# Four passes over gathered rows: every tile gathered by GpSimd, none by SyncE's one-row transfers

## The chip, the cores and the metric

The kernel runs on one core of one Trainium2 chip. The metric is the device time of one execution in microseconds (us); the profile is a separate execution, taken by the hardware profiler. Engines are named as in the profile: PE (TensorE matmul), PEld (its weight load), DVE (VectorE), ACT (ScalarE), POOL (GpSimd) and SP (SyncE). SP computes nothing: it issues transfers and passes semaphores on.

## The reference

Four graph layers work one after the other on 12500 nodes of 128 features, with the same 200000 edges, which are sorted by their destination `dst`:

```
h = relu(layernorm(x)); x = x + GCN(h)          # two convolutions: 128 -> 256 -> 128
h = relu(layernorm(x)); x = x + L1(h)           # total - segment_sum(h[src], dst), normalised, linear
h = relu(layernorm(x)); x = x + weightedGCN(h)  # edge weights in the messages and in the degrees
h = relu(layernorm(x)); x = x + GAT(h)          # projections of both ends, batch norm, silu, edge softmax
```

What costs time is in each layer `segment_sum(rows[src], dst)`: for each edge a row of a table in HBM, by a random number `src`, is fetched, and rows with one destination are added up.

## The kernel before

The edges are cut into 1563 tiles of 128 edges (`NT`). A gather fetches one tile: an indirect DMA, issued by POOL, whose 128 partitions each receive the row that one number of `idx_tab` names. The kernel has five passes over all tiles (numbers 0 to 4), each in a block of its own, with a barrier of all engines between blocks:

- passes 0, 1 and 2 (`pass_in_parts`) fetch from `table16`, whose rows of 384 bf16 numbers (768 bytes) hold each value in three parts. ACT builds one-hot matrices, PE multiplies them with the rows into PSUM windows of 128 nodes, DVE evicts windows;
- pass 3 (`pass_with_weights`) fetches 512-byte rows of `table`; DVE builds the weighted one-hot matrices, ACT evicts;
- pass 4 fetches 520-byte rows of `ptable` and sends its sums to HBM; a last block multiplies them out, then come the final norm and the output.

Between the passes stand short blocks with the layers' linear algebra and norms, which store the next table.

In a pass tiles go in groups of eight (`GT`), 196 groups (`TGROUPS`), through a ring in SBUF of eight groups (`RGROUPS`; four in pass 4). Three engines keep the ring going:

- POOL (`gather_tiles`) issues a group's gathers one by one; from group 8 on it first waits until `s_free` says that the slots are empty;
- SP (`relay_rows`) waits until a group has landed and counts it up in `s_landed`, two groups (`LEAD`) ahead, for PE; then it waits until PE's products of the oldest group are done and counts `s_free` up, for POOL;
- PE waits for `s_landed` every eight products.

In passes 0 to 3 POOL doesn't fetch all tiles. Of each sixth group from the eighth on (`SIDE`: 31 groups, 8 to 188) it leaves out the last tile. SP fetches that tile's 128 rows by 128 transfers of one row each (`side_rows`), cut into six portions of some 21 rows, one after each `s_free` that it gives: it loads 32 row numbers at once into registers (line 502, four loads for a tile), and each transfer (line 506) takes its address from one of them. The numbers come from two small tables in SBUF (`side_of`), which the first block loads and multiplies by the row's size (lines 835, 973 and 975). SP waits for the tile by a semaphore of its own (`s_side`, line 470), clears it (line 471) and only then hands the group over (line 472).

Of the kernel before, what the change touches and what calls it, by code (L numbers as in the profile page):

```python
# [5 lines left out]
P = 128  # L6
F = 128
GT = 8
SLOTS = 4 * GT
READY_STEP = 4  # L10
RGROUPS = 8
LEAD = 2
SIDE_FIRST, SIDE_EVERY = 8, 6
SIDE_LOAD = 32
Z_RGROUPS = 4
# [3 lines left out]
NPARTS = 3  # L19
# [37 lines left out]
def gnn_kernel(nc, x, src, dst, edge_weight, node_vec1, L0_W1, L0_b1, L0_W2, L0_b2, L1_W, L1_b, L2_W, L2_b,  # L57
# [21 lines left out]
    NTAB = NI + BODY  # L79
    SIDE = list(range(SIDE_FIRST, TGROUPS - RGROUPS + LEAD + 1, SIDE_EVERY))  # L80
    SIDE_SPAN = SIDE_EVERY * GT * P
    SIDE_BASE = (SIDE_FIRST + 1) * GT * P - SIDE_SPAN
    assert SIDE_FIRST == RGROUPS and RGROUPS - SIDE_EVERY == LEAD and SIDE_BASE + len(SIDE) * SIDE_SPAN <= E
    CHUNKS = NW // CW
# [24 lines left out]
    with ctx:  # L109
# [76 lines left out]
        score_tab = ew_tab[:, 0:NI]  # L186
        side_tab = sb("side_numbers", [64 + len(SIDE), P], i32)
        side_of = [side_tab[64 * k:64 * k + len(SIDE), :] for k in range(2)]
        rows_all = sb("rows", [13, max(7 * SCW, NI // 2, PLAN_HALVES * PLAN_WORDS)])
# [247 lines left out]
        s_free = sem("rows_free")  # L437
        s_side = sem("side_rows")

        def tiles_of(g):  # L440
            return min(GT, NT - g * GT)

        def has_side(no, g):

            return no < PASSES - 1 and g in SIDE

        def landed_count(no, g):

            return 16 * sum(tiles_of(k) - has_side(n, k) for n in range(no + 1)
                            for k in range(g % RGROUPS, g + 1 if n == no else TGROUPS, RGROUPS))  # L450

        def gather_tiles(pool, no, tab, slots, groups, width):

            freed = no * (TGROUPS - RGROUPS)
            for g in range(TGROUPS):
                if g >= groups:
                    pool.wait_ge(s_free, freed + g - groups + 1)
                for k in range(tiles_of(g) - has_side(no, g)):
                    t = g * GT + k
                    pool.indirect_dma_start(  # L460
                        out=slots[:, t % (groups * GT), 0:width], out_offset=None, in_=tab,
                        in_offset=bass.IndirectOffsetOnAxis(ap=idx_tab[:, t // P, t % P:t % P + 1], axis=0),
                    ).then_inc(gathered[g % RGROUPS], 16)

        def relay_rows(sp, no, groups, lead, s_done, done0, fetch_side=None):

            def landed(g):
                sp.wait_ge(gathered[g % RGROUPS], landed_count(no, g))
                if has_side(no, g):
                    sp.wait_ge(s_side, 16 * P)  # L470
                    sp.sem_clear(s_side)
                sp.sem_inc(s_landed[no], 1)  # L472

            for g in range(lead):
                landed(g)
            for g in range(TGROUPS):
                if g + lead < TGROUPS:
                    landed(g + lead)
                if g + groups < TGROUPS:
                    if g % 4 == 0:  # L480
                        releases = table_values(sp, RELEASE, g, 4, NI)
                    sp.wait_ge(s_done, releases[g % 4] + done0)
                    sp.sem_inc(s_free, 1)
                    if fetch_side:
                        fetch_side(sp, g)

        def side_rows(no, tab, slots, width, kind, row_bytes):

            flat, size = tab.rearrange("n f -> (n f)").unsqueeze(0), row_bytes // width

            numbers = []

            def fetch(sp, g):
                k, j = g // SIDE_EVERY, g % SIDE_EVERY
                if k >= len(SIDE):
                    return
                t = SIDE[k] * GT + GT - 1
                for e in range(j * P // SIDE_EVERY, (j + 1) * P // SIDE_EVERY):
                    if e % SIDE_LOAD == 0:
                        numbers.clear()  # L500
                        words = [nc.alloc_registers(f"side{no}_{k}_{e + i}", engines=[SP]) for i in range(SIDE_LOAD)]
                        nc.regs_load(words, side_of[kind][k:k + 1, e:e + SIDE_LOAD])
                        numbers.extend(nc.snap(word, engines=[SP], donate=True, min_val=0, max_val=(N - 1) * row_bytes,
                                               guaranteed_mod_val=0, out_of_modulus=row_bytes) for word in words)
                    at = numbers[e % SIDE_LOAD] // size
                    sp.dma_start(slots[e:e + 1, t % RSLOTS, 0:width], flat[:, bass.ds(at, width)]).then_inc(s_side, 16)

            return fetch

# [61 lines left out]
        def pass_in_parts(no, from_acc, sums_of, finish, count_weights=False):  # L571
# [3 lines left out]
            with nc.Block() as block:  # L575
# [4 lines left out]
                @block.sync  # L580
                def _(sp):
                    relay_rows(sp, no, RGROUPS, LEAD, s_prod, items0, side_rows(no, table16, ring16, NPARTS * F, 0, 2 * NPARTS * F))

# [72 lines left out]
        def pass_with_weights(no):  # L656
# [3 lines left out]
            with nc.Block() as block:  # L660
# [4 lines left out]
                @block.sync  # L665
                def _(sp):
                    relay_rows(sp, no, RGROUPS, LEAD, s_prod, items0, side_rows(no, table, ring32, F, 1, 4 * F))

# [96 lines left out]
        with nc.Block() as block:  # L765
# [58 lines left out]
            def _(sp):  # L824
# [6 lines left out]
                else:  # L831
                    sp.sem_inc(s_last, 16)
                side_src = src[SIDE_BASE:SIDE_BASE + len(SIDE) * SIDE_SPAN].rearrange("(k s) -> k s", s=SIDE_SPAN)[:, SIDE_SPAN - P:]
# [52 lines left out]
            def _(act):  # L886
# [65 lines left out]

                act.wait_ge(s_dve, 16)
                nc.scalar.activation(deg_r, deg, ACT.Sqrt).then_inc(s_cnt, 1)
# [9 lines left out]
            def _(dve):  # L964
# [25 lines left out]
                dve.wait_ge(s_starts, 1)  # L990
                step = Steps(dve, s_dve, 4, 10)
                step(nc.vector.tensor_tensor(bound[:, 0:NW], bank[5][:, 0:NW], wplus1[:, 0:NW], ALU.add))
# [82 lines left out]

                step = Steps(dve, s_dve, 4 + 10, 3)
                dve.wait_ge(s_degrees, 1)
# [18 lines left out]
            def _(pe):  # L1096
# [5 lines left out]
                last.then_inc(s_counted, 1)  # L1102
                pe.wait_ge(s_dve, 4)
                nc.tensor.matmul(bank[5][:, 0:NW], first, tile_cnt[:, 1:NW + 1], start=True, stop=True).then_inc(s_starts, 1)
# [886 lines left out]
```

## Time and profile before

| | |
|---|---|
| time of an execution, median of 3 | 14196.16 us (14169.2 to 14197.04) |
| profiled execution, first to last instruction | 11157.3 us |
| POOL busy | 8098.3 us, 73% of the span |
| PE, PEld busy | 4270.1 us (38%), 2948.2 us (26%) |
| DVE, ACT busy | 3430.3 us (31%), 3212.6 us (29%) |
| gathers (DMA_INDIRECT, line 460) | 4596 + 1532 + 1563 |
| one-row transfers (line 506) | 11904 + 3968 |

The profiled execution's own time is known as its span alone; what lies around it isn't in the profile. The median of the three timed executions is 3038.9 us above the span. The busy shares are means over passes and the blocks between them, so a bound has to be read stage by stage. What SP issues isn't counted as busy, nor is POOL's sequencer between two gathers.

### The profile page before, as it was taken

How to read it: one execution, taken by the hardware profiler on the slowest of the kernel's cores; microseconds unless marked ns; L12 is line 12 of the kernel's file. 1: busy time of each engine (PE TensorE's matmuls, PEld its weight loads, DVE VectorE, ACT ScalarE, POOL GpSimd, SP SyncE). 2: the span in 40 equal slices, each digit the busy share in tenths (PEclk: the TensorE clock that was granted, in tenths of full speed). 3: DMA queues.
4: the chain of work that ended last, by engine and by line, in shares of the span. 5: the costliest groups of instructions: out<-in, count | busy, mean ns of one | idle time of the engine just before them, and what ended most of it. 6: DMA issues, size and time to landing. Idle time of an engine off the chain costs nothing. (4 is left out here: it accounts for less than half of the span.)

```text
span 11157.3 us, 112702 instructions
## 1 busy us (share of the span) xinstructions
PE 4270.1 (38%) x19462; PEld 2948.2 (26%) x19462; DVE 3430.3 (31%) x7386; ACT 3212.6 (29%) x7261; POOL 8098.3 (73%) x8241
## 2 busy tenths in 40 slices
PE   1222222342222233333333433343464333443687
PEld 0111111121111112111111333333353333333576
DVE  4000001110001112000001422222245677777898
ACT  3333333343333334333333300000031111111465
POOL 4777777657777775777777677777766777777676
PEclk5555555665555555555555555556675555555899
DMA  4333333233333333333333222222214555555444
GB/s 105 81 81 81 81 81 81 76 88 81 81 81 81 81 81 102 81 81 81 81 81 81 59 54 54 54 54 54 54 48 148 159 162 163 166 166 170 149 167 134
DMA packets 702798, 1071.72 MB, mean 96 GB/s; under 512 B 164740, under 2 KB 547065, under 8 KB 675209
## 3 DMA queue, kind: packets, MB, share of 16 engines
q0 software_dynamic: 323616, 664.87, 23.0%
q10 hardware_dynamic: 247712, 225.10, 6.1%
q1 hardware_dynamic: 130793, 174.77, 4.9%
q14 instruction: 501, 4.10, 0.1%
q8 instruction: 176, 2.88, 0.1%
HBM read 904.67 MB, written 161.05 MB: 96 GB/s over the span
## 5 line engine op out<-in xcount | busy, mean ns | idle before, releaser
L460 POOL DMA_INDIRECT big<-table_parts,tile_cols x4596 | 4348.0, 946 | 1563.2 <-issue 1400.2
L641 PE MATMUL psum<-big 128*128 x4992 | 1722.0, 505 | 3998.4 <-SPq L472 3044.2
L641 PEld LDWEIGHTS psum<-big 128*128 128x128 bf16 x4992 | 670.0, 141 | 4980.6 <-issue 2814.6
L460 POOL DMA_INDIRECT big<-ptable,tile_cols x1563 | 1496.6, 957 | 498.4 <-issue 476.0
L460 POOL DMA_INDIRECT big<-table,tile_cols x1532 | 1454.6, 949 | 469.5 <-issue 467.0
L596 ACT ACTIVATE big<-big,ones 128x2048 bf16<-128x2048 bf16 x312 | 624.4, 2001 | 3573.5 <-PE psum L641 2381.1
L589 ACT ACTIVATE big<-iota_col,dl_tab 128x128 bf16<-128x128 f32 x4992 | 1490.7, 387 | 32.9 <-PEq L765 12.5
L1656 PE MATMUL psum<-acc,big 128*128 x3328 | 785.0, 419 | 1205.5 <-DVE big L1632 1193.4
L618 DVE TENSOR_REDUCE acc<-psum 128x128 f32<-128x384 f32 (+1 forms) x196 | 109.7, 560 | 3558.1 <-PE psum L644 1783.4
L713 PE MATMUL psum<-big 128*128 x3328 | 754.6, 419 | 1158.3 <-SPq L472 619.7
L1656 PEld LDWEIGHTS psum<-acc,big 128*128 128x128 f32 x3328 | 701.8, 315 | 1288.5 <-issue 1288.2
L713 PEld LDWEIGHTS psum<-big 128*128 128x128 f32 x3328 | 704.8, 323 | 1209.5 <-SPq L472 534.3
L676 DVE TENSOR_SCALAR big<-iota_col,dl_tab,ew_tab 128x128 f32<-128x128 f32 x1664 | 438.8, 365 | 1476.1 <-PE psum L713 1469.4
L1609 DVE TENSOR_REDUCE wide<-big 128x128 f32<-128x2048 f32 x208 | 766.1, 3683 | 3.2 <-ACT big L1683 3.2
L1632 DVE SCALAR_TENSOR_TENSOR big<-big,sc,psum 128x130 f32<-128x130 f32 x1664 | 515.9, 343 | 552.9 <-SPq L472 294.7
L618 DVE TENSOR_REDUCE big<-psum 128x128 f32<-128x384 f32 x98 | 54.7, 558 | 1722.2 <-PE psum L641 1722.1
L692 ACT COPY acc<-psum 128x128 f32<-128x128 f32 x98 | 26.0, 266 | 1858.4 <-PE psum L713 1849.0
L1868 PE MATMUL psum<-big 128*128 128x129 f32 x3328 | 543.4, 297 | 38.5 <-POOL big L1789 36.5
L1788 POOL TENSOR_TENSOR big<-big,tile_cols 128x2048 f32<-128x2048 f32 x104 | 376.0, 3615 | 119.4 <-ACT big L1829 119.2
L1868 PEld LDWEIGHTS psum<-big 128*128 128x128 f32 x3328 | 425.1, 193 | 68.2 <-issue 52.7
L1683 ACT ACTIVATE big<-big 128x2048 f32<-128x2048 f32 x104 | 199.6, 1920 | 712.1 <-DVE wide L1613 707.6
L644 PE MATMUL psum<-big 128*128 128x3 bf16 x1664 | 352.5, 212 | 0.0
(301 smaller groups left out, 4278.8 us busy)
## 6 DMA issues: line engine op xcount, KB each, us to landing
big<-table_parts SPq DMA_DIRECT2D x11904, 0.8 KB
big<-dl_rows ACTq DMA_DIRECT2D x104, 1024.0 KB
zrows<-big ACTq DMA_DIRECT2D x104, 1024.0 KB, 5.5
big<-zrows SPq DMA_DIRECT2D x104, 1024.0 KB, 4.9
big<-table_parts,tile_cols POOLq DMA_INDIRECT x4596
big<-table SPq DMA_DIRECT2D x3968, 0.5 KB
table_parts<-big SPq DMA_DIRECT2D x42, 672.0 KB, 3.5
big<-ptable,tile_cols POOLq DMA_INDIRECT x1563
```

The lines of the kernel that those rows point to most:

```text
L460: pool.indirect_dma_start(out=slots[:, t % (groups * GT), 0:width], out_offset=None, in_=tab, in_offset=bass.IndirectOffsetOnAxis(ap=idx_t ...
L589: last = nc.scalar.activation(apart_flat[:, u * P:(u + 1) * P], iota_col[:], ACT.Abs, bias=dl_tab[:, col:col + 1], scale=-1.0)
L596: nc.scalar.activation(half, apart_flat, ACT.Relu, bias=ones[:, 0:1], scale=-1.0).then_inc(s_onehot, 1)
L641: last = nc.tensor.matmul(held, m, rows_t, start=False, stop=False, skip_group_check=True)
L644: last = nc.tensor.matmul(held, m, ew_parts[:, q * HALF + u, :], start=False, stop=False, skip_group_check=True)
L676: last = nc.vector.tensor_scalar(wide_onehot[:, q % 2 * HALF + u, :], iota_col[:], dl_tab[:, col:col + 1], ew_tab[:, col:col + 1], ALU.is_ ...
L713: last = nc.tensor.matmul(held, wide_onehot[:, q % 2 * HALF + u, :], rows_t, start=False, stop=False, skip_group_check=True)
L1609: nc.vector.tensor_reduce(part[:, k, :], rows_of, AX.X, ALU.add).then_inc(s_part, 1)
L1632: last = nc.vector.scalar_tensor_tensor(zbuf[:, h, u, 0:ACW], dyn(ring_flat, slots[u], ACW), in_win[:, h, u:u + 1], bank[n % Z_BANKS][:, 0 ...
L1656: last = nc.tensor.matmul(bank[n % Z_BANKS][:, 0:ACW], onehot_t[:, q % 2, u * P:(u + 1) * P], dyn(acc_flat, at[u], ACW), start=True, stop= ...
L1788: nc.gpsimd.tensor_tensor(m[:, :, 0:F], m[:, :, 0:F], over_f(weights_of(q), HALF), ALU.mult)
L1868: nc.tensor.matmul(dyn(sums_at, at[u], SCW), onehot[:, q % 2 * HALF + u, :], msg[q % MSGS][:, u, 0:SCW], start=False, stop=False, skip_gro ...
```

## The change

POOL gathers all tiles of all groups in all passes. `relay_rows` only hands groups over and slots back. `side_rows`, its registers, semaphore and two number tables go, and with them their two loads and two multiplications in the first block. Counts of semaphores that those steps had raised are lowered to match. Nothing of what PE, ACT or DVE compute in the passes changes.

```diff
 def landed_count(no, g):
-    return 16 * sum(tiles_of(k) - has_side(n, k) for n in range(no + 1)
+    return 16 * sum(tiles_of(k) for n in range(no + 1)
                     for k in range(g % RGROUPS, g + 1 if n == no else TGROUPS, RGROUPS))
 ...
     for g in range(TGROUPS):
         if g >= groups:
             pool.wait_ge(s_free, freed + g - groups + 1)
-        for k in range(tiles_of(g) - has_side(no, g)):
+        for k in range(tiles_of(g)):
 ...
-def relay_rows(sp, no, groups, lead, s_done, done0, fetch_side=None):
+def relay_rows(sp, no, groups, lead, s_done, done0):
     def landed(g):
         sp.wait_ge(gathered[g % RGROUPS], landed_count(no, g))
-        if has_side(no, g):
-            sp.wait_ge(s_side, 16 * P)
-            sp.sem_clear(s_side)
         sp.sem_inc(s_landed[no], 1)
 ...
             sp.wait_ge(s_done, releases[g % 4] + done0)
             sp.sem_inc(s_free, 1)
-            if fetch_side:
-                fetch_side(sp, g)
-
-def side_rows(no, tab, slots, width, kind, row_bytes):
-    ...
-                nc.regs_load(words, side_of[kind][k:k + 1, e:e + SIDE_LOAD])
-    ...
-            sp.dma_start(slots[e:e + 1, t % RSLOTS, 0:width], flat[:, bass.ds(at, width)]).then_inc(s_side, 16)
 ...
-                for to in side_of:
-                    sp.dma_start(to, side_src).then_inc(s_last, 16)
 ...
-                dve.wait_ge(s_last, 64)
-                nc.vector.tensor_scalar(side_of[0], side_of[0], 2 * NPARTS * F, None, ALU.mult)
-                step = Steps(dve, s_dve, 0, 4)
-                step(nc.vector.tensor_scalar(side_of[1], side_of[1], 4 * F, None, ALU.mult))
+                dve.wait_ge(s_last, 32)
+                step = Steps(dve, s_dve, 0, 3)
```

On POOL, in the middle of pass 0, this stands before: gathers of 128 rows of 384 numbers, the first of each group behind its wait for `s_free` (rows_free).

```order
L460 DMA big<-table_parts,tile_cols 128x384 x7
L460 DMA big<-table_parts,tile_cols 128x384 [waits rows_free]
L460 DMA big<-table_parts,tile_cols 128x384 x6
L460 DMA big<-table_parts,tile_cols 128x384 [waits rows_free]
L460 DMA big<-table_parts,tile_cols 128x384 x7
```

And now, at the same place (line 447 of the changed kernel is the same gather):

```order
L447 DMA big<-table_parts,tile_cols 128x384 x7
L447 DMA big<-table_parts,tile_cols 128x384 [waits rows_free]
L447 DMA big<-table_parts,tile_cols 128x384 x7
L447 DMA big<-table_parts,tile_cols 128x384 [waits rows_free]
L447 DMA big<-table_parts,tile_cols 128x384 x7
```

The group that had seven gathers has eight; this comes 31 times in a pass.

On SP, also in pass 0, this stands before: 64 transfers of one row, number loads, the hand-over waits (`gathered0` to `gathered7` are the semaphores of the gathers' groups, `product_done` that of PE).

```order
L512 TENSOR_LOAD rows [waits gathered6]
L506 DMA big<-table_parts 1x384 [waits product_done]
L506 DMA big<-table_parts 1x384 x10
L502 TENSOR_LOAD side_numbers
L506 DMA big<-table_parts 1x384 x10
L506 DMA big<-table_parts 1x384 [waits gathered7,product_done]
L506 DMA big<-table_parts 1x384 x21
L471 ISA [waits side_rows,gathered0]
L502 TENSOR_LOAD side_numbers [waits product_done]
L506 DMA big<-table_parts 1x384 x21
```

And now, where line 471 of the changed kernel is what was line 512:

```order
L471 TENSOR_LOAD rows [waits product_done,gathered7,gathered0,gathered1,gathered2]
L471 TENSOR_LOAD rows [waits product_done,gathered3,gathered4,gathered5,gathered6]
L471 TENSOR_LOAD rows [waits product_done,gathered7,gathered0,gathered1,gathered2]
L471 TENSOR_LOAD rows [waits product_done,gathered3,gathered4,gathered5,gathered6]
L471 TENSOR_LOAD rows [waits product_done,gathered7,gathered0,gathered1,gathered2]
```

Between two loads of four release numbers nothing is left on SP but the waits and counts.

## Rows read from the trace of the kernel before

**Rows 1.** The stages: us of the window, busy time (x instructions), PEclk, DMA share, GB/s.

```profile
267.00:2183.00 1916.00, 570.42 (x1671) 218.59 (x1670) 126.78 (x388) 704.37 (x1767) 1449.22 (x1532) 0.55 0.30 81
2307.00:4222.00 1915.00, 571.92 (x1671) 218.98 (x1670) 172.82 (x580) 703.96 (x1765) 1448.11 (x1532) 0.55 0.30 81
4284.00:6202.00 1918.00, 611.90 (x3327) 303.83 (x3328) 109.83 (x290) 704.84 (x1768) 1450.29 (x1532) 0.54 0.30 81
6324.00:8247.00 1923.00, 764.93 (x3326) 706.70 (x3327) 438.58 (x1664) 51.38 (x194) 1454.61 (x1532) 0.59 0.21 54
8394.00:10368.00 1974.00, 779.57 (x3306) 696.93 (x3307) 1419.95 (x2681) 230.43 (x308) 1496.57 (x1563) 0.57 0.56 163
```

**Rows 2.** Line 460, the gathers of each pass: min/median/max ns, first and last start.

```profile
L460 POOL DMA_INDIRECT big<-table_parts,tile_cols x1532: 942/946/1317, 267.0 to 2182.0; - x192
L460 POOL DMA_INDIRECT big<-table_parts,tile_cols x1532: 942/946/1045, 2306.6 to 4220.9; - x192
L460 POOL DMA_INDIRECT big<-table_parts,tile_cols x1532: 942/946/1445, 4284.5 to 6200.5; - x192
L460 POOL DMA_INDIRECT big<-table,tile_cols x1532: 940/944/1089, 6324.4 to 8245.1; - x192
L460 POOL DMA_INDIRECT big<-ptable,tile_cols x1563: 940/944/1213, 8394.5 to 10366.1; - x196
```

**Rows 3.** What POOL waited for: us in total, times, longest.

```profile
POOL big L460 <- issue: 2343.2, 7686, 0.3
POOL big L460 <- POOLq L765: 63.0, 1, 63.0
```

**Rows 4.** POOL in order of time, in pass 0 and at its end.

```profile
999.61 0.95 POOL L460 DMA_INDIRECT big<-table_parts,tile_cols  x1 [0.30 <-issue]
1000.86 0.95 POOL L460 DMA_INDIRECT big<-table_parts,tile_cols  x1 [0.30 <-issue]
...
2181.95 0.95 POOL L460 DMA_INDIRECT big<-table_parts,tile_cols  x1 [0.30 <-issue]
2190.67 6.84 POOL L1159 TENSOR_TENSOR big<-acc,dinv 128x896 f32<-128x896 f32 x3 [7.77 <-POOLq L575]
```

**Rows 5.** SP's one-row transfers and number loads, whole trace.

```profile
L506 SPq DMA_DIRECT2D big<-table_parts x11904: 219/225/342, 301.7 to 6138.5; - x199
L506 SPq DMA_DIRECT2D big<-table x3968: 224/225/338, 6359.4 to 8182.7; - x199
L502 SPq TENSOR_LOAD <-side_numbers x496: 1865/2124/2383, 299.6 to 8169.7; - x166
```

**Rows 6.** SP in order of time in pass 0: a run without a load, and a long stretch.

```profile
999.86 1.81 SPq L506 DMA_DIRECT2D big<-table_parts  x6
939.78 126.35 SPq L506 DMA_DIRECT2D big<-table_parts  x272
```

**Rows 7.** What SP waited for between 900 and 2100 us.

```profile
SPq L472 <- DMA big<-table_parts,tile_cols: 92.7, 83, 2.9
SPq L470 <- DMA big<-table_parts: 27.3, 20, 1.7
```

**Rows 8.** What PE waited for in pass 0.

```profile
PE psum L641 <- SPq L472: 993.7, 140, 8.0
PE psum L641 <- issue: 219.8, 34, 7.7
PE psum L641 <- SPq L471: 131.4, 22, 6.3
```

**Rows 9.** DVE at the start of the first block, in order of time.

```profile
4.71 0.59 DVE L971 TENSOR_SCALAR is_node<-node_id 128x98 f32<-128x98 f32 x1 [3.62 <-POOL big L789]
6.47 0.21 DVE L973 TENSOR_SCALAR side_numbers<-side_numbers 31x128 int32<-31x128 int32 x1 [1.17 <-DMA side_numbers<-in_src]
6.95 0.17 DVE L976 TENSOR_SCALAR big<-big 128x13 int32<-128x13 int32 x1
```

More of the change, by code:

```diff
@@ L12 @@
 LEAD = 2
-SIDE_FIRST, SIDE_EVERY = 8, 6
-SIDE_LOAD = 32
 Z_RGROUPS = 4
@@ L79, in gnn_kernel @@
     NTAB = NI + BODY
[L80 to L83, printed above, removed]
     CHUNKS = NW // CW
@@ L186, in gnn_kernel @@
         score_tab = ew_tab[:, 0:NI]
-        side_tab = sb("side_numbers", [64 + len(SIDE), P], i32)
-        side_of = [side_tab[64 * k:64 * k + len(SIDE), :] for k in range(2)]
         rows_all = sb("rows", [13, max(7 * SCW, NI // 2, PLAN_HALVES * PLAN_WORDS)])
@@ L437, in gnn_kernel @@
         s_free = sem("rows_free")
-        s_side = sem("side_rows")
         def tiles_of(g):
             return min(GT, NT - g * GT)
-        def has_side(no, g):
-            return no < PASSES - 1 and g in SIDE
         def landed_count(no, g):
-            return 16 * sum(tiles_of(k) - has_side(n, k) for n in range(no + 1)
+            return 16 * sum(tiles_of(k) for n in range(no + 1)
                             for k in range(g % RGROUPS, g + 1 if n == no else TGROUPS, RGROUPS))
@@ L483, in relay_rows @@
                     sp.sem_inc(s_free, 1)
-                    if fetch_side:
-                        fetch_side(sp, g)
-        def side_rows(no, tab, slots, width, kind, row_bytes):
[L489 to L501, printed above, removed]
-                        nc.regs_load(words, side_of[kind][k:k + 1, e:e + SIDE_LOAD])
-                        numbers.extend(nc.snap(word, engines=[SP], donate=True, min_val=0, max_val=(N - 1) * row_bytes,
-                                               guaranteed_mod_val=0, out_of_modulus=row_bytes) for word in words)
-                    at = numbers[e % SIDE_LOAD] // size
-                    sp.dma_start(slots[e:e + 1, t % RSLOTS, 0:width], flat[:, bass.ds(at, width)]).then_inc(s_side, 16)
-            return fetch
         def table_values(eng, tab, start, n, largest):
@@ L581, in _ @@
                 def _(sp):
-                    relay_rows(sp, no, RGROUPS, LEAD, s_prod, items0, side_rows(no, table16, ring16, NPARTS * F, 0, 2 * NPARTS * F))
+                    relay_rows(sp, no, RGROUPS, LEAD, s_prod, items0)
                 @block.scalar
@@ L666, in _ @@
                 def _(sp):
-                    relay_rows(sp, no, RGROUPS, LEAD, s_prod, items0, side_rows(no, table, ring32, F, 1, 4 * F))
+                    relay_rows(sp, no, RGROUPS, LEAD, s_prod, items0)
                 @block.vector
@@ L832, in _ @@
                     sp.sem_inc(s_last, 16)
-                side_src = src[SIDE_BASE:SIDE_BASE + len(SIDE) * SIDE_SPAN].rearrange("(k s) -> k s", s=SIDE_SPAN)[:, SIDE_SPAN - P:]
-                for to in side_of:
-                    sp.dma_start(to, side_src).then_inc(s_last, 16)
                 sp.wait_ge(s_pad, 4)
@@ L951, in _ @@
                         ln.relu(act, t - 1, (t - 1) % 2)
-                act.wait_ge(s_dve, 16)
+                act.wait_ge(s_dve, 15)
                 nc.scalar.activation(deg_r, deg, ACT.Sqrt).then_inc(s_cnt, 1)
@@ L990, in _ @@
                 dve.wait_ge(s_starts, 1)
-                step = Steps(dve, s_dve, 4, 10)
+                step = Steps(dve, s_dve, 3, 10)
                 step(nc.vector.tensor_tensor(bound[:, 0:NW], bank[5][:, 0:NW], wplus1[:, 0:NW], ALU.add))
@@ L1074, in _ @@
                         keep_dl(t - 2)
-                step = Steps(dve, s_dve, 4 + 10, 3)
+                step = Steps(dve, s_dve, 3 + 10, 3)
                 dve.wait_ge(s_degrees, 1)
@@ L1102, in _ @@
                 last.then_inc(s_counted, 1)
-                pe.wait_ge(s_dve, 4)
+                pe.wait_ge(s_dve, 3)
                 nc.tensor.matmul(bank[5][:, 0:NW], first, tile_cnt[:, 1:NW + 1], start=True, stop=True).then_inc(s_starts, 1)
```

## The prediction

> **What bounds the kernel now.** I read the stages first, then what ends the waits of each engine in them; the chain of waits on the page covers only the last block and says nothing of the passes. The reader is to see in the stages [rows 1] that four windows of 1915 to 1923 us have the same number of gathers, 1532, and very different work on the other engines: PE goes from 570 to 765 us, ACT from 704 down to 51, DVE from 110 up to 439. Their lengths don't follow any of it. They follow POOL: 1448 to 1455 us busy in all four. The DMA engines have a share of 0.21 to 0.30 there, and of 0.56 in pass 4, so they aren't the bound.
>
> The gathers themselves [rows 2] give the pitch from one to the next: (2182.0 - 267.0) / 1531 = 1.2508 us in pass 0, 1914.3 / 1531 = 1.2504 in pass 1, 1916.0 / 1531 = 1.2515 in pass 2, 1920.7 / 1531 = 1.2545 in pass 3 and 1971.6 / 1562 = 1.2622 in pass 4, which has no one-row transfers beside it. A pitch is 0.95 us of gather and 0.30 us of its own sequencer [rows 4]. What POOL waited for [rows 3] has 7686 such gaps of at most 0.3 us put down to issue, one wait at the barrier before pass 0, and no wait for `s_free`: the ring of eight groups never runs full. And the pass ends right behind POOL: its next instruction in the next block starts 7.8 us after its last gather [rows 4]. So in passes 0 to 3 the path is POOL's chain of gathers, and one gather more is one pitch more.
>
> SP is the second in line. A one-row transfer takes 0.225 us [rows 5], but six take 1.81 us, so the pitch between them is (1.81 - 0.225) / 5 = 0.317 us [rows 6]. A tile costs SP 128 x 0.317 + 4 x 2.124 us of number loads [rows 5] = 49.1 us. POOL gives it 47 gathers for that (six groups of eight less one): 47 x 1.251 = 58.8 us. SP is used to 84% by this alone; over a long stretch it issues 272 rows in 126.35 us, 59.5 us for 128 [rows 6], POOL's own pace, and it waits 120 of 1200 us, nearly all of it for landings [rows 7]. It keeps up. PE's waits that end with SP's lines 472 and 471 [rows 8] are only the hand-over of rows that PE has long been free for.
>
> **The change part by part.**
>
> Added: 31 gathers in each of four passes. In passes 0 to 2, 3 x 31 x 1.251 = 116.3 us; in pass 3, 31 x 1.2545 = 38.9 us. Together 155.2 us. The lower bound for a pitch is a gather alone, 0.94 us [rows 2], should the sequencer's gap hide (124 x 0.94 = 117 us), the upper the pitch of pass 4 (124 x 1.2622 = 156.5 us). I take 155, since every gather in those passes has its gap. Nothing hides it: POOL has no wait to give up.
>
> Removed on SP: 15872 one-row transfers, 496 number loads and 124 clears. They lie beside POOL's chain and are worth 0 there. Could their going make POOL's pitch shorter? The nearest rows say no: the median gather is 946 ns in passes 0 to 2, 944 in pass 3 and 944 in pass 4 without them. At the most 2 ns x 4596 = 9 us come back; I take 0, because pass 3 has them too and shows 944.
>
> What is late next: SP hands over a group as soon as its last gather has landed, where it might first have had up to 21 rows to issue. PE gets rows a little sooner, and still waits for POOL: it is busy 570 to 765 us of some 1920 [rows 1]. Slots are given back sooner; POOL doesn't wait for them. The last side group is the 188th, so the end of a pass is as before.
>
> In the first block two loads and two multiplications go. DVE waits 1.17 us for the side numbers, and from the end of line 971 (5.30) to line 976 (6.95) 1.65 us could go, if the last numbers of `dst` have landed by then [rows 9]; between 0 and -1.65 us I take -1.
>
> The sum is +154 us: the profiled execution would go from 11157.3 to about 11311 us. That span is 3038.9 us below the median of the timed executions, and the trace doesn't tell where those lie. I take them as unchanged: 14196 + 154 = 14350 us. If instead all of them lay in the gathers' pitch, it would be 1.251 + 3038.9 / 7691 = 1.646 us in the timed executions, and the 124 gathers 204 us: 14400 us. That is the other end for the same mechanism.
>
> On this the Trainium skill's page "Runtime: NRT & Kernel Launch" (The ~15µs preamble/postamble breakdown) has about 9 to 15 us around a kernel. The 3038.9 us here are two hundred times that; by that rule most of them lie inside the execution, which speaks for the higher end and also for the first rival below.
>
> **The rivals.**
>
> B, faster: SP, not POOL, sets the pace in the timed executions. The place is the portion of 21 rows before each hand-over. SP decides as soon as a tile costs it more than 58.8 us, that is from (58.8 - 8.5) / 128 = 0.393 us a row, 24% above the 0.317 us of the trace. Were all the 3038.9 us due to it, a tile would cost 58.8 + 3038.9 / 124 = 83.3 us, 0.584 us a row, and with the transfers gone the time would fall to 11157.3 + 154, about 11310 us; at half of it, 12830 us. For it speaks that SP has only 16% in reserve and that 3 ms have no place yet. Against it: in the trace SP waits 10% of the time and POOL never waits for slots [rows 3, 7], the 15872 transfers vary only from 219 to 342 ns [rows 5], and nothing shown makes an execution without the profiler slower in SP alone.
>
> The Trainium skill's page "DMA: Bandwidth & Descriptors" gives 512 sequencer cycles for such a transfer on this generation (section "Why a DMA increments its semaphore by 16 and not by 1", its table's column on previous generations), which at the 1.2 GHz of the Trainium skill's page "Trainium Kernel Development and Optimization" (NeuronCore Architecture) is an estimate of 0.427 us, beyond the 0.393 of the rival; the trace has 0.225 us, and here the measurement decides.
>
> C, no change: the gathers' issue isn't what binds, or less of it. To leave the time alone POOL's pitch would have to fall to 1.251 x 1532 / 1563 = 1.226 us once SP's rows are off the DMA queues, and the time would be 14195 us. For it: the one-row transfers share the DMA engines with the gathers. Against it: that share is 0.30, and pass 4 has the same gather of 944 ns at a share of 0.56 and no row transfers [rows 1, 2].
>
> The Trainium skill's page "DMA: Bandwidth & Descriptors" also says (Issuing engines are not separate DMA queues) that issuing from several engines at once only saves the sequencer's issue time, usually small beside the transfer. By that rule the side rows were worth little and C would hold; in the trace issue is the larger part, 1.25 us of every gather at a DMA share of 0.30.
>
> That the change doesn't do what it says is excluded by the order: eight gathers stand where seven stood.
>
> **How the numbers follow.** The forecast, slower by 154 to 204 us, gets 0.80; B 0.11; C 0.09. The predicted time is 14350 us. A measurement of this kernel can't tell less than about 0.2% (28 us) from no change. The forecast's own range is 14310 to 14430 us: 154 less the 38 us of the hidden gaps and a little for the median, up to 204 and the same. That holds about 0.76; to leave out no more than 2 in 10 I reach down over C, to 14180. The range is 14180 to 14430 us; B lies outside. Faster by over 0.2%: B's 0.11 and 0.02 of C, 0.13. Within 0.2%: the rest of C, 0.07. Slower: 0.80.
>
> **What the profile of the changed kernel would show.** Right: 1563 gathers in each of the first four passes, at a pitch of 1.25 us, windows of about 1954 to 1962 us instead of 1915 to 1923, POOL's idle time still put down to issue, pass 4 as before, no line 502 or 506, and the first gather at about 266 us. SP would wait for landings nearly all the time. Wrong: a pitch of 1.23 us or less (C); waits of POOL for slots, which would mean that PE or SP had become the bound; or a span of about 11311 us with a timed median that falls towards it, which would show that the missing 3 ms were SP's (B). A span of about 11311 us and a timed median some 200 us higher would put them into the gathers.

## The result and the profile after

The changed kernel took 12869.92 us (median of 4 runs, 12863.67 to 12872.75) beside 14186.72 us for the kernel before (4 runs, 14169.2 to 14197.04). The ratio is 0.9069, 95% interval [0.9052, 0.9086]: faster by 9.3%, where 1.1% slower was forecast, and far below the range.

One thing has to be known to read any number below. The same kernel before takes 11156 to 11189 us in some jobs on the chips and 14187 to 14201 us in others (medians), and all its runs of one job lie within about 0.5%. A job is one session on one chip, in which several kernels are timed beside one another. I call these the 11.2 jobs and the 14.2 jobs. The timed runs of the forecast come from a 14.2 job, the profile of before from an 11.2 job. A ratio is always to runs of before in the same job, and where times of different jobs are compared, the jobs are of one kind.

The windows of the five passes of the changed kernel in its 14.2 job, with the columns of [rows 1]:

```profile
279.00:2479.00 2200.00, 493.77 (x1664) 206.48 (x1662) 122.69 (x380) 707.59 (x1764) 1480.34 (x1563) 0.56 0.26 70
2606.00:4808.00 2202.00, 495.83 (x1664) 207.67 (x1664) 166.36 (x564) 707.55 (x1767) 1480.37 (x1563) 0.56 0.26 70
4875.00:7100.00 2225.00, 545.20 (x3248) 281.02 (x3248) 104.61 (x281) 693.01 (x1740) 1484.46 (x1563) 0.57 0.26 69
7232.00:9450.00 2218.00, 639.41 (x3269) 585.75 (x3270) 426.54 (x1632) 49.78 (x189) 1481.31 (x1563) 0.60 0.18 47
9609.00:12064.00 2455.00, 786.14 (x3280) 701.31 (x3280) 1407.14 (x2662) 228.28 (x305) 1490.60 (x1563) 0.55 0.45 131
```

The number of gathers rose from 1532 to 1563 as forecast, but a pass takes 2200 to 2225 us, not 1954 to 1962. The gathers themselves are what they were in [rows 2]:

```profile
L447 POOL DMA_INDIRECT big<-table_parts,tile_cols x4689: 940/946/1440, 278.9 to 7099.2; - x196
L447 POOL DMA_INDIRECT big<-table,tile_cols x1563: 938/944/1094, 7233.0 to 9449.4; - x196
L447 POOL DMA_INDIRECT big<-ptable,tile_cols x1563: 938/944/1221, 9609.8 to 12063.1; - x196
```

What is new is a wait that [rows 3] does not have, first on POOL, then on SP, with total, times and longest ("remote": the trace doesn't show which engine's instruction ended the wait):

```profile
POOL big L447 <- issue: 2319.3, 7512, 2.5
POOL big L447 <- SPq L467: 1560.5, 298, 17.5
```

```profile
SPq L467 <- remote: 6835.6, 407, 48.9
SPq L467 <- DVE big L1586: 1462.9, 145, 25.6
```

POOL waits 1560.5 us for slots that SP gives back at line 467, and SP waits at its wait for PE's count, where in [rows 7] it waited for landings. The prediction named this as the mark of "wrong".

The same two views of the kernel before in a 14.2 job (run e15, 14201.13 us) were the missing piece, since the profile that the forecast was read from is of the other kind of job:

```profile
279.00:2854.00 2575.00, 561.81 (x1648) 215.16 (x1648) 123.02 (x379) 696.72 (x1751) 1456.85 (x1532) 0.54 0.23 60
2983.00:5532.00 2549.00, 560.34 (x1648) 214.80 (x1648) 165.80 (x560) 695.93 (x1750) 1455.53 (x1532) 0.54 0.23 61
5604.00:8153.00 2549.00, 601.03 (x3248) 297.30 (x3246) 105.27 (x280) 692.57 (x1739) 1457.19 (x1532) 0.53 0.23 61
8287.00:10800.00 2513.00, 754.20 (x3262) 696.06 (x3262) 428.80 (x1632) 50.13 (x189) 1453.62 (x1532) 0.56 0.16 41
10954.00:13400.00 2446.00, 786.43 (x3281) 701.83 (x3282) 1411.75 (x2665) 228.46 (x306) 1499.29 (x1563) 0.55 0.45 131
```

```profile
POOL big L460 <- SPq L483: 3004.2, 591, 17.4
POOL big L460 <- issue: 2207.7, 7026, 2.0
```

So the 3038.9 us lay inside the passes. Against [rows 1], passes 0 to 3 take 659, 634, 631 and 590 us more, pass 4 takes 472 more, all the rest 56: 3042 us. POOL is as busy as in [rows 1] (1457 for 1449 us in pass 0) and waits 3004.2 us for slots, which is nearly the whole difference. The change then takes 375, 347, 324 and 295 us off passes 0 to 3, 1341 us, and nothing off pass 4 (2455 for 2446) or outside the windows (1566.9 for 1567.4). So the spans differ by 1332.5 us, and the medians at the top by 1317.

SP's rows in the 14.2 job, first between 900 and 2100 us and then over the whole trace (min/median/max ns):

```profile
L506 SPq MOVE big<-table_parts x1932: 1/29/1409, 900.0 to 2099.9; - x194
L506 SPq DMA_DIRECT2D big<-table_parts x1932: 1/228/1421, 900.1 to 2099.9; - x194
```

```profile
L506 SPq DMA_DIRECT2D big<-table_parts x11904: 1/228/1421, 317.2 to 8135.7; - x199
```

and in an 11.2 job, between the same times:

```profile
L506 SPq MOVE big<-table_parts x2610: 29/29/38, 902.3 to 2099.8; - x187
L506 SPq DMA_DIRECT2D big<-table_parts x2610: 224/225/318, 902.4 to 2099.8; - x187
```

The reader is to see that the medians hardly differ (228 for 225 ns) and the number of rows does: 1932 against 2610 in the same 1200 us, 0.621 us a row with all that SP does beside it. The longest of a transfer is 1421 ns where it was 342 [rows 5]. SP is not slower all the time: from one transfer to the next it takes 322 ns in the median, where it was 318, but it halts again and again. Of its 4060 steps from one instruction to the next in this stretch, those behind a load left out, 411 take 0.6 to 0.8 us and 148 take 1.3 to 1.5 us, against 15 and 17 in the profile of before (counted from the traces' records). SP has 12.2 us of waits in that stretch, where it had 120 [rows 7]:

```profile
SPq L470 <- DMA big<-table_parts: 12.2, 11, 1.4
```

SP is full, and a tile costs it 128 x 0.621 = 79.5 us, number loads and halts included, while POOL would need 58.8 us for the six groups.

### The profile page after: what moved, and what is told of

The parts are those of the page before. It is cut to its first block and busy times, and to the rows that moved or that the text cites. A ratio compares the mean times of both kernels' runs of the same rounds, so it can differ in the third digit from the quotient of the medians.

```text
span 12866.9 us, 80456 instructions
## 1 busy us (share of the span) xinstructions
PE 3963.6 (31%) x19462; PEld 2811.3 (22%) x19462; DVE 3421.9 (27%) x7384; ACT 3223.1 (25%) x7261; POOL 8214.4 (64%) x8365
## 5 line engine op out<-in xcount | busy, mean ns | idle before, releaser
L447 POOL DMA_INDIRECT big<-table_parts,tile_cols x4689 | 4445.7, 948 | 2348.6 <-issue 1398.7
L600 PE MATMUL psum<-big 128*128 x4992 | 1507.0, 459 | 5013.4 <-issue 2719.2
L447 POOL DMA_INDIRECT big<-table,tile_cols x1563 | 1481.7, 948 | 738.2 <-issue 468.6
L600 PEld LDWEIGHTS psum<-big 128*128 128x128 bf16 x4992 | 628.2, 131 | 5806.9 <-issue 4232.7
L672 PE MATMUL psum<-big 128*128 x3328 | 638.9, 365 | 1583.0 <-issue 876.4
L672 PEld LDWEIGHTS psum<-big 128*128 128x128 f32 x3328 | 592.8, 273 | 1630.5 <-issue 1271.9
L1822 PEld LDWEIGHTS psum<-big 128*128 128x128 f32 x3328 | 427.6, 194 | 66.5 <-issue 51.3
```

Source lines behind the costliest of these rows:

```text
L447: pool.indirect_dma_start(out=slots[:, t % (groups * GT), 0:width], out_offset=None, in_=tab, in_offset=bass.IndirectOffsetOnAxis(ap=idx_t ...
L600: last = nc.tensor.matmul(held, m, rows_t, start=False, stop=False, skip_group_check=True)
L672: last = nc.tensor.matmul(held, wide_onehot[:, q % 2 * HALF + u, :], rows_t, start=False, stop=False, skip_group_check=True)
L1822: nc.tensor.matmul(dyn(sums_at, at[u], SCW), onehot[:, q % 2 * HALF + u, :], msg[q % MSGS][:, u, 0:SCW], start=False, stop=False, skip_gro ...
```

## Experiments

**Are the time and the sum reproducible: the kernel before, unchanged (e1, e13, e15), and the changed kernel again (e5).** No edit.

> The kernel before, unchanged. Question: where do the 3039 us stand by which its timed executions exceed its profiled span? Theory H (hand-over): in the timed executions the counts of PE's finished products reach SP late, POOL waits for slots, and SP's portions of 21 row transfers lengthen each turn; then the span here is near 14190 us, gathers keep their median of 0.95 us, and POOL waits some 3000 us for SP's line 472 in the passes. Rival O (outside): the span is again about 11160 us and the rest lies around it. Rival P (pitch): the span is near 14190 and the gathers' own pitch is 1.6 us.

> The kernel before. Where it takes 14187 us, theory R (instructions and counts of all engines drain at a limited rate there) expects SP's own instructions stretched to some 0.7 us in bursts, as the half-reduced version showed, about 2500 us a pass, POOL with some 3000 us of waits for slots, and few of the counts' records; the gathers still at 0.95 us. Where it takes 11187, as e1.

> As e13. Where it takes 14187 us: POOL waits some 3000 us for slots, SP's instructions are stretched to some 0.7 us in bursts, a pass takes about 2500 us.

> The changed kernel, unchanged, beside the kernel before. In the last call the kernel before took 11187 us, its profiled span, where it had taken 14187 us beside the changed kernel; so the time of one and the same kernel differs by 27% between jobs. Theory S (a state of the chip or of the job in which semaphore counts come late, not a property of the kernels): if the kernel before is near 11187 us here, the changed one is 155 us above it, near 11342 us, as the version with LEAD = 6 was, and POOL has no waits for slots; if the kernel before is near 14187, the changed one is near 12870 again. Rival K (the changed kernel itself makes the counts late, since SP waits instead of issuing): 12870 us whatever the kernel before takes.

Before took 11186.67 us (ratio to the runs of before beside it 1.0 [0.999, 1.0009]), 11155.69 (0.9998) and 14201.13 (1.0001 [0.9986, 1.0016]). So both kinds of jobs are stable, and the kernel is the same in them. The profiled execution of e15 took 14201.16 us, no longer than its other seven. e1 expected a 14.2 job and its marks; they came with e15: 3004 us of waits, gathers at 949 ns (median) and not at a pitch of 1.6 us. The changed kernel in an 11.2 job: 11348.87 us beside 11187.68, ratio 1.0143 [1.0126, 1.016], 161 us more where the sum said 154. (Between the two profiled executions it is 188.6 us, 178 of them in passes 0 to 3 and 11 in pass 4.) Its passes 0 and 4 and POOL's gaps before its gathers:

```profile
267.00:2231.00 1964.00, 568.81 (x1671) 217.58 (x1672) 126.78 (x388) 704.81 (x1768) 1487.23 (x1563) 0.55 0.29 78
8570.00:10555.00 1985.00, 781.59 (x3304) 698.84 (x3304) 1419.54 (x2679) 230.24 (x306) 1508.19 (x1563) 0.57 0.56 162
```

```profile
POOL big L447 <- issue: 2381.4, 7810, 0.3
```

The change has the opposite sign in the two kinds of jobs. There is no wait for slots here, as the prediction's own marks of "right" had it.

**Gathers and transfers both (e3, e10, e14, e16).** The kernel before, but POOL gathers every tile, and SP still issues all 15872 one-row transfers, 320 bytes each, into memory that nobody reads:

```diff
+        side_dump = sb("side_dump", [P, 160], bf16)
 ...
-            return 16 * sum(tiles_of(k) - has_side(n, k) for n in range(no + 1)
+            return 16 * sum(tiles_of(k) for n in range(no + 1)
 ...
-                for k in range(tiles_of(g) - has_side(no, g)):
+                for k in range(tiles_of(g)):
 ...
-                    sp.dma_start(slots[e:e + 1, t % RSLOTS, 0:width], flat[:, bass.ds(at, width)]).then_inc(s_side, 16)
+                    sp.dma_start((side_dump[e:e + 1, :] if width > F else side_dump[e:e + 1, :].bitcast(f32)), flat[:, bass.ds(at, 160 if width > F else 80)]).then_inc(s_side, 16)
```

> POOL gathers every tile, as in the changed kernel, and SP issues its 15872 row transfers as before, at the same places and with the same number loads and waits, but into a scratch tile and of 320 bytes each; nobody uses them. Theory H: the row transfers cost their time on SP, so this is as slow as before plus at most the 155 us of the 31 gathers a pass: 14200 to 14400 us. Rival: what the change gains comes from somewhere else than SP's transfers (the tile's landing, say, that PE no longer waits for): near 12900.

> POOL gathers every tile and SP issues the 15872 row transfers into a scratch tile. 11344 us where the kernel before takes 11187, as much as the changed kernel without them. Where it takes 14187: theories R and T1 both say that the transfers cost what they cost before, plus the 124 gathers: 14340 us; if the late landing of a tile that PE waits for was the cost, 12870.

> POOL gathers every tile and SP issues the 15872 transfers into a scratch tile. 11310 to 11344 us where the kernel before takes 11160 to 11190. Where it takes 14187: theory R expects 14340 (the transfers cost what they cost there, plus the gathers) give or take 150; if PE's wait for the tile's late landing was the cost, 12870.

> As e14. Where the kernel before takes 14187 us: 14340 give or take 150 by theory R, 12870 if PE's wait for the tile was the cost.

In 11.2 jobs: 11344.05 us, ratio 1.0139 [1.0122, 1.0156], 1.0127 [1.0084, 1.0171] and 1.0137 [1.0108, 1.0166], the same as the changed kernel without any transfer (1.0143). There the transfers are worth nothing beside POOL. In a 14.2 job: 14536.14 us beside 14195.91, ratio 1.0236 [1.0193, 1.0278]. Against the changed kernel's 12870 us that is 1666 us for 15872 transfers and their number loads, 105 ns each, though no byte that they bring is used. So what the change gains comes from the transfers being gone, not from PE getting its rows another way. It is 340 us above before, more than the 154 to 204 of my sum for the gathers and more than the 14340 us, give or take 150, that was expected: the slots go back later still.

```profile
POOL big L462 <- SPq L485: 3168.1, 552, 18.8
```

```profile
L508 SPq DMA_DIRECT2D side_dump<-table_parts x1875: 1/228/1398, 900.1 to 2098.8; - x188
```

**Half of the side tiles (e6).** The kernel before with 16 of 31 side tiles:

```diff
-            return no < PASSES - 1 and g in SIDE
+            return no < PASSES - 1 and g in SIDE[0::2]
 ...
-                if k >= len(SIDE):
+                if k >= len(SIDE) or k % 2:
```

> The kernel before with every second side tile given back to POOL: 16 of 31 groups keep their tile on SP, 15 gathers more in each of passes 0 to 3. Theory S, where the kernel before takes 11187 us: 60 gathers by 1.254 us, 75 us slower, 11262 us. Where the kernel before takes 14187 us: SP's portions hold the late hand-overs up half as often, so about half of the difference of the two kernels is gone, 13500 us. Rival (one side tile in the ring is enough to spoil the hand-over): near 14187 there.

In a 14.2 job: 13582.6 us beside 14190.34, ratio 0.957 [0.9538, 0.9602], where the middle of the two kernels is about 13530. POOL waits 2312.3 us for slots. The gain grows with the number of rows that go. No step is seen at this one point between the two kernels.

**More lead for PE (e2, e7).** The changed kernel, with six groups handed over ahead:

```diff
-LEAD = 2
+LEAD = 6
```

> The changed kernel with LEAD = 6: SP may hand over six groups ahead instead of two before it has to wait for PE's products of the oldest. Theory H: PE and SP take turns because SP stands at the wait for products while landed groups aren't handed over; with more lead the stalls of POOL (about 250 us in each of passes 0 to 3) mostly go, 12870 falls by 600 to 1000 us. Rival D (the counts are late whatever SP does, and the ring of eight groups is what they drain): no change, within 1% of 12870.

> The changed kernel with LEAD = 6 once more, for a job in which semaphore counts come late. Where the kernel before takes 11187 us it is again at 11342, by which it differs from the changed kernel (11349) by nothing. Where the kernel before takes 14187 us, theory H: SP no longer stands at the wait for products with landed groups in hand, PE and SP stop taking turns, and the time falls clearly below the changed kernel's 12870, to 11350 to 12300. Rival D (the late counts drain the ring of eight groups whatever the lead is): 12870.

11342.0 us in an 11.2 job (1.0141 [1.0124, 1.0157]) and 12852.64 in a 14.2 job (0.9055 [0.9025, 0.9086]): both as the changed kernel. Theory H, that SP and PE take turns through the small lead and each waits for the other, is out. POOL's wait stays the same with it:

```profile
POOL big L447 <- SPq L467: 1558.8, 272, 17.6
```

**Few transfers, many number loads (e4, e9, e12).** As the kernel with both, but each portion has 4 transfers instead of 21 or 22, each with a load of 32 numbers of its own ahead (2976 transfers and 2976 loads in all):

```diff
-                    sp.wait_ge(s_side, 16 * P)
+                    sp.wait_ge(s_side, 16 * 4 * SIDE_EVERY)
 ...
-                    if e % SIDE_LOAD == 0:
+                    if e >= e0 + 4:
+                        break
+                    if True:
 ...
```

> As e3, but each portion is four number loads and four transfers instead of 21 transfers and under one load: SP is held as long (about 9.8 us against 8.2), with 2976 transfers instead of 15872. Theory H, where SP's time is what costs: as slow as e3 or some 10% of its excess more, about 14300 to 14600. Rival T (the transfers' traffic, descriptors and semaphore writes make the counts late): a fifth of e3's excess over the changed kernel, about 13150 us.

> SP held as long as by 21 transfers in each portion, by four loads and four transfers, 2976 transfers in all; POOL gathers every tile. 11684 us where the kernel before takes 11187. Where it takes 14187: theory R, with 8900 instructions instead of 32200, says 12870 + 1475 x 0.28 = 13280 us or, as SP's time alone costs 335 us already in the other job, somewhat more, to 13500; rival T1 says at least 14340, as e3.

> As e9 (four loads and four transfers a portion): 11680 us where the kernel before takes 11160 to 11190. Where it takes 14187: about 13300 to 13500 us by theory R, at least 14340 by T1, 12870 plus the 335 us of the other jobs, 13200, by T2.

In 11.2 jobs SP is now over its measure: 11683.78 us (1.0441 [1.0423, 1.0458]) and 11680.19 (1.0459 [1.0415, 1.0503]), and POOL waits for it, 1.1 us at a time:

```profile
POOL big L462 <- SPq L485: 443.2, 402, 3.4
```

In a 14.2 job it takes 13065.96 us beside 14201.3, ratio 0.9205 [0.9168, 0.9243], only 196 us more than the changed kernel. The theory that what counts is SP's time as an 11.2 job shows it (14340 us or more) is refuted: here SP is full even in an 11.2 job, by loads of 2.1 us, and yet this kernel is 1135 us faster than before in a 14.2 job. It issues few instructions. The two other theories had the direction and not the size: R, a limited rate of instructions and counts, said 13300 to 13500 us, and T2 13200. That T2, the transfers on the queues, is the only cost falls with the next experiment. What makes up the 196 us isn't worked out.

**Idle counts on SP (e8, e11, e17).** The changed kernel, with no transfer at all, but 38 semaphore counts that nobody waits for after every slot given back in passes 0 to 3 (28576 in all); in e17 there are 76 and a clear.

```diff
                     sp.sem_inc(s_free, 1)
+                    if no < PASSES - 1:
+                        for k in range(38):
+                            sp.sem_inc(s_idle, 1)
```

> The changed kernel, with 38 counts more on SP behind each slot that it gives back in passes 0 to 3: 28576 instructions of 17 ns at a pitch near 65 ns, on a semaphore that nobody waits for; no transfers. They hold SP for about 2.5 us of the 10 us of a group, so where the kernel before takes 11187 us nothing is late and the time stays at 11349. Where it takes 14187: theory R (there the instructions and counts of all engines drain at a limited rate, and everything that is waited for queues behind them; each row transfer cost two instructions and some four counts) says that these 28576 instructions and as many counts cost a good part of the 1320 us that the row transfers cost, 13400 to 14100 us. Rival T1 (SP's time before the hand-over is what costs, 8.2 us a portion): 2.5 us are three tenths of that, but in each group, about 13000 to 13300. Rival T2 (the transfers on the DMA queues cost): 12870.

> As e8 (28576 idle counts on SP): 11327 us where the kernel before takes 11160 to 11190. Where it takes 14187: 13400 to 14100 us by theory R (instructions and counts of all engines drain at a limited rate there), 13000 to 13300 by T1 (SP's time), 12870 by T2 (the transfers on the DMA queues).

> The changed kernel, with 76 idle semaphore counts and one clear on SP for every slot that it gives back in passes 0 to 3, where the kernel with idle counts had 38. In a job where the kernel before takes 14200 us, the traces have 4144, 4021 and 4082 SP instructions in 1200 us for the kernel before, for both and for 38 idle counts, so 3.4 per us each time, with SP hardly waiting. Theory P (SP's instructions pass at about 3.4 per us in such a job, whatever they are): a slot costs SP 76 + 1 + 3 = 80 instructions / 3.4 = 23.5 us, 188 slots in four passes 17700 us where the changed kernel has 8845: about 21000 to 22500 us. Theory L (each idle count adds to the time what it added with 38 of them, 540 / 28576 = 19 ns): 13950 us, 13800 to 14200. In a job where the kernel before takes 11187 us, 76 counts cost SP 2 x 2.3 = 4.6 us of the 10.0 us of a slot: 11330 to 11350 us by both.

In 11.2 jobs: 11327.33 us (1.0143 [1.0092, 1.0194]), and 11342.45 (1.0146 [1.0107, 1.0184]) with the double. They cost nothing, SP has room. In a 14.2 job: 13409.94 us beside 14201.3, ratio 0.9448 [0.9418, 0.9477], which is 540 us above the changed kernel, 19 ns for each count. That is at the very low end of what R expected (13400 to 14100), and outside T1 (13000 to 13300) and T2 (12870). The counts move no data, so it is refuted that only the rows' traffic can cost time. The counts in the 11.2 job and then in the 14.2 job, between 900 and 2100 us:

```profile
L471 SPq EVENT_SEMAPHORE  x4560: 17/17/17, 901.9 to 2098.9; - x199
```

```profile
L471 SPq EVENT_SEMAPHORE  x3856: 1/17/1408, 899.9 to 2100.0; - x193
```

```profile
POOL big L448 <- SPq L468: 2140.8, 459, 17.4
```

This is the clearest picture of the cause. The last row is POOL's wait in the 14.2 job. Worked out from the trace's records, 38 such counts take SP 2.2 to 2.6 us in the 11.2 job, and in the 14.2 job 3.3 to 49.6 us, median 10.9, together 8345 us of the four passes. Most of that is halts: 4783 of the 28576 counts last over 0.6 us themselves, and others start only 0.7 or 1.4 us after the one before. Between the halts SP goes on at its old pace. These are two neighbouring stretches of e11, 1008 to 1024.3 us and 1024.3 to 1025.7 us:

```profile
L471 SPq EVENT_SEMAPHORE  x20: 4/687/713, 1008.7 to 1024.3; - x20
L471 SPq EVENT_SEMAPHORE  x22: 9/17/17, 1024.3 to 1025.6; - x22
```

Between 900 and 2100 us SP has no wait at all. The eight gathers of a slot take POOL 10.0 us. So SP, with nothing to do but count, is the bound there.

**The same counts on another engine (e18).** The changed kernel, with 38 idle counts on DVE after each of the 98 windows of passes 0 to 2.

```diff
                         finish(dve, w, sums)
+                        for k in range(38):
+                            dve.sem_inc(s_idle, 1)
```

> The changed kernel, with 38 idle semaphore counts on DVE after each of the 98 windows of passes 0 to 2 (11172 in all); DVE is busy 123 of 2200 us there. In a job where the kernel before takes 14200 us: theory own (each engine's instructions pass at a limited rate of their own): DVE needs 38 x 0.29 = 11 us of the 22.4 us of a window, and the time stays at 12870, up to 60 us more. Theory shared (the rate is one for all engines of the core, so that an idle count costs the same wherever it is issued): 11172 x 19 ns = 210 us more, 13080, 13020 to 13250. In a job where the kernel before takes 11187 us: 11345 by both.

This came in an 11.2 job: 11351.57 us, ratio 1.0154 [1.0115, 1.0193], as both theories had it there. It tells them apart only in a 14.2 job, and so does e17. The kept traces say something on it all the same. In e15 all engines together pass 7578 instructions between 900 and 2100 us, and 10166 between 6300 and 7500 us, where PE has 4079 instead of 1692 (pass 2 in the windows above); SP passes 4144 and 4299. In e11 it is 7971 and 10356 (6000 to 7200 us), and SP 4082 and 4036. So SP's pace isn't its share of one limit on the instructions of all engines. A common limit on something else, on semaphore counts for example, isn't excluded.

## Why the prediction was wrong

**The step that failed** is "That span is 3038.9 us below the median of the timed executions, and the trace doesn't tell where those lie. I take them as unchanged". They lay in the passes, nearly all in POOL's wait for slots (3004 us in e15), and 2514 of them in the four passes that the change touches. With it fell "Removed on SP: ... worth 0 there": true in the kind of job of the trace (e3 against e5), but 1341 us in that of the times. The forecast added a term read from a trace of one kind to a time of the other; what made the two differ was the job and not the profiler.

**The sum itself** held where its profile holds: +154 us forecast, +161 measured in an 11.2 job by the medians (188.6 by the two profiles), windows of 1961 to 1964 us for 1954 to 1962, no line 506, POOL put down to issue throughout, the rest of the span as before (1510.9 for 1511.3 us). Lead, earlier hand-over and the one-row transfers' share of the queues were worth nothing there, as said.

**The rival B** had the mechanism: SP sets the pace in the timed executions, from 0.393 us a row on, number loads apart. The 14.2 job has (79.5 - 8.5) / 128 = 0.555. Its working, a tile at 83.3 us if all the 3038.9 were SP's, comes near: SP needs 79.5 us for a tile, and six groups of pass 0 take 2575 x 6 / 196 = 78.8 us. It came out too high because 472 of the 3038.9 us lie in pass 4, which has no rows. I gave it 0.11, on the ground that the transfers vary only from 219 to 342 ns and that nothing shown slows SP alone; both were facts about the other kind of job. It also expected the time to fall to 11310 us if all of it were SP's. It fell to 12870. That this is near its half-way figure of 12830 is chance: the excess over the 11.2 jobs was 3000 us (14187 - 11187), and 1521 stay when the rows are gone, 470 of them in pass 4, because something else is late then, which B didn't have.

**What the rows cost in a 14.2 job.** Counted from the trace's records between 900 and 2100 us, SP passes 4144 instructions in the kernel before (e15), 4021 with both (e16) and 4082 with idle counts (e11), and hardly waits: 3.4 per us each time, be they transfers of 228 ns or counts of 17 ns. This is a mean over halts of 0.7 or 1.4 us and stretches at the old pace. It is much the same in the other passes: 3.4 to 3.65 per us over 1200 us of each of passes 1 to 3 in these three runs. In an 11.2 job the kernel before passes 5595 in that stretch and has waits left. A row costs two, a MOVE and the transfer: 256 instructions at 3.4 per us are 75 of the 79.5 us. That the cost goes by the number of instructions and not by bytes or by the durations that SP has in an 11.2 job is what e11, e15 and e16 together speak for; the double of e17 would have tested it, and didn't meet a 14.2 job. e12 fits, as far as it goes: it passes 1496 instructions in 1200 us, and its 2976 long loads are not stretched, 2132 ns in the median in an 11.2 job (e4) and 2092 in the 14.2 job (min/median/max ns):

```profile
L507 SPq TENSOR_LOAD <-side_numbers x2976: 1865/2132/2267, 299.1 to 8742.4; - x199
```

```profile
L507 SPq TENSOR_LOAD <-side_numbers x2976: 2/2092/2238, 314.6 to 9647.5; - x199
```

**What is late next.** With the rows gone SP has 240 instructions in 1200 us and isn't full. There the counts of PE come late. The changed kernel in pass 0, in order of time:

```profile
359.81 2.74 PE L600 MATMUL psum<-big 128*128 x8 [18.94 <-issue]
...
382.99 2.72 PE L600 MATMUL psum<-big 128*128 x8 [20.43 <-issue]
...
404.57 2.00 ACT L555 ACTIVATE big<-big,ones 128x2048 bf16<-128x2048 bf16 x1 [38.02 <-remote]
404.64 0.13 PEld L600 LDWEIGHTS psum<-big 128*128 128x128 bf16 x2 [19.63 <-SPq L456]
404.64 2.74 PE L600 MATMUL psum<-big 128*128 x8 [18.94 <-SPq L456]
404.78 0.94 POOL L447 DMA_INDIRECT big<-table_parts,tile_cols  x1 [6.11 <-SPq L467]
```

and in an 11.2 job:

```profile
369.70 2.13 PE L600 MATMUL psum<-big 128*128 x6
...
371.93 2.00 ACT L555 ACTIVATE big<-big,ones 128x2048 bf16<-128x2048 bf16 x1 [13.22 <-PE psum L600]
```

Each batch is 16 products, and ACT may fill a buffer again when PE has done the batch in it. By the order of the items, ACT at 404.57 needs the batch that ended at 362.55 (359.81 + 2.74), and starts 42.0 us behind it. It, PE's next batch and POOL's next gather all start from 404.57 to 404.78, within 0.21 us of one another. In the 11.2 job ACT starts at 371.93, 0.1 us behind the end of the batch at 371.83 (369.70 + 2.13). Over pass 0 ACT starts 16.3 us (median of 102) behind the PE work that it waits for, and 0.1 us in the 11.2 job. With a lead of six groups it is 37.5 us (e7), and the kernel takes as long as with two. In e15 and e11, where SP is full, ACT's median is 0.1 us: so the two latenesses seem to take each other's place rather than add up. Why they do is not shown.

On the Trainium skill: its page "DMA: Bandwidth & Descriptors" (Issuing engines are not separate DMA queues) says that issuing from several engines only saves the sequencer's issue time, usually small. The 11.2 jobs show a small effect too, with e3 equal to e5; in the 14.2 jobs the issuing on SP costs 105 ns a row, and the measurement decides. The estimate of 0.427 us a transfer that I made from that page's table is wrong in both: 225 and 228 ns in the traces, while the pace is 0.32 and 0.62 us a row.

**What stays open** is what makes a job one or the other. Chip 8 gave both kinds, in different jobs. It isn't TensorE's clock: the granted one is 0.599 for the changed kernel in its 14.2 job and 0.596 in an 11.2 job (0.575 and 0.596 for the kernel before), and PE is busy no longer in the passes of e15 than in [rows 1] (562 for 570 us in pass 0). It isn't the DMA engines, whose share is 0.23 in pass 0 where the 11.2 job has 0.30. The traces of 14.2 jobs lack most records of semaphore updates (the window of pass 0 of the changed kernel: 3959 for the 25968 of e5). This hints at a limit on the way of such events or of their records; whether it is the cause or goes along with it no run shows. No run had instructions left out on PE, which would test the lateness of its counts.

No version beat both kernels in both kinds of jobs. Before is the best in 11.2 jobs; in 14.2 jobs the changed kernel is, and with a lead of six the ratio to before is the same within the interval.

## What to carry to other kernels

Before a term is set to zero "because the trace shows it hidden", hold the span of the trace against the timed median. Where they are 27% apart, as here, the trace may not be of the state that is timed, and each engine that is near its measure there (SP was at 84%) has to be taken as a candidate for the bound. A helper engine that relays semaphores for others should issue few instructions: in the 14.2 jobs each took some 0.29 us of SP's time in the mean, a count of 17 ns as well as half of a row's fetch, while in the 11.2 jobs they were free until SP was full.

## What the hardware showed unexpectedly

- One program takes 11187 us or 14200 us, by the job, with about 0.5% at most between runs of one job. The granted clock doesn't explain it (0.599 and 0.596 for the changed kernel in the two kinds).
- In the long kind a full SP passes 3.4 to 3.65 instructions per us in the mean, with halts of 0.7 and 1.4 us between stretches at the old pace. A count of 17 ns (median) takes 0.29 us of its time (8345 us / 28576) instead of 0.06 (2.3 us / 38). With 2.4 times as many instructions on PE the pace is the same.
- There, with SP not full, ACT starts 16.3 us in the median and up to 53 us behind the PE work that it waits for (pass 0 of the changed kernel), and in the place shown ACT, PE and POOL then start within 0.21 us of one another.
- In the 11.2 jobs 15872 transfers of one row beside 6252 gathers cost nothing measurable (1.0139 against 1.0143).
